# Reordering the head of a gated mixture-of-experts attention kernel: keys ahead of x, weight maxima in two rounds, weight halves at other places

## What is computed

```python
# xattn(batch=ctx, latent=layernorm(x))
weights = softmax((latent @ Wq.T) @ (batch @ Wk.T).T / sqrt(128))
x = x + tanh(g_xattn[0]) * weights @ (batch @ Wv.T)
# ffn(layernorm(x)), tokens n = 64*128, 4 blocks of sequences behave alike
logits = normalise(h) @ normalise(sim_matrix) - sigmoid(gates)
w = softmax(where(mask > 0, relu(logits), -inf))        # over the 16 experts
q = sum_e w[:, e] * (h @ q_proj[e])                     # k and v likewise
o = softmax(q @ k.T / sqrt(128)) @ v                    # within a sequence
x = x + tanh(g_ffn[0]) * sum_e (w[:, e] * o) @ o_proj[e]
```

## Time and profile before

| | |
|---|---|
| median of 3 runs | 885.28 us (885.21 to 885.91) |
| time of the profiled execution | 885.93 us |
| its span, first to last instruction | 884.1 us |
| TensorE products | 828.6 us busy, 94% of the span |
| VectorE | 613.5 us, 69% |
| GpSimd | 552.1 us, 62% |
| ScalarE | 519.3 us, 59% |
| mean granted TensorE clock | 0.992 |

### The profile page before, as it was taken

The page is one execution under the profiler, slowest core; times in us unless marked ns, Lnnn a source line. Parts: engine busy times, 40 slices in busy tenths (PEclk is TensorE's granted clock), DMA queues, the critical chain, the costliest instruction groups (busy, mean ns, idle before and its releaser), DMA issues.

```text
span 884.1 us, 16223 instructions
## 1 busy us (share of the span) xinstructions
PE 828.6 (94%) x4344; PEld 458.8 (52%) x4344; DVE 613.5 (69%) x1575; ACT 519.3 (59%) x1148; POOL 552.1 (62%) x588
## 2 busy tenths in 40 slices
PE   4579999999999999999999999999999999999976
PEld 3445555555555555555555555555555555545432
DVE  3777567777685867768676786867677676766545
ACT  3555657565665756566575656656575565656353
POOL 2264567575675757567575756657575765857464
PEclk9999999999999999999999999999999999999988
DMA  8753554453645555364654536464463636466342
GB/s 224 188 191 107 188 196 156 165 183 127 225 128 198 191 174 176 115 217 144 198 176 175 198 104 221 133 203 166 175 202 121 228 103 216 151 205 214 97 154 72
DMA packets 58531, 150.49 MB, mean 170 GB/s; under 512 B 5568, under 2 KB 22144, under 8 KB 58496
## 3 DMA queue, kind: packets, MB, share of 16 engines
q1 hardware_dynamic: 57776, 150.00, 50.3%
q10 hardware_dynamic: 720, 0.08, 0.1%
HBM read 145.34 MB, written 4.72 MB: 170 GB/s over the span
## 4 chain that ended last, share of the span: by engine, by line
PE 33%; issue 29%; POOL 28%; DVE 5%; ACT 3%; POOLq 1%; DMA 1%; ACTq 0%; DVEq 0%
POOL stage L457 13%; POOL zq L452 9%; PE acc_q L890 7%; PE acc_k L890 7%; PE acc_v L890 7%; PE acc_o L906 6%; POOL rstd L437 2%; POOL norm L446 1%; POOL rstd L425 1%; DVE zo_full L753 1%; DVE zq_full L743 1%; PE oT_p L982 1%; PE m L928 1%; PE m L1029 1%; DMA sim_sb<-in_L_ffn_sim_matrix_dram 1%
## 5 line engine op out<-in xcount | busy, mean ns | idle before, releaser
L452 POOL TENSOR_TENSOR zq<-zq_full,zq 128x512 f16<-128x512 f32 x192 | 224.8, 1172 | 218.6 <-ACT zq L505 218.6
L505 ACT ACTIVATE zq<-zq_full 128x512 f16<-128x512 f32 x256 | 161.0, 629 | 201.0 <-DVE zq_full L743 195.6
L457 POOL TENSOR_TENSOR stage<-zo_full,stage 128x512 f16<-128x512 f32 x208 | 240.7, 1160 | 58.2 <-ACT stage L513 58.2
L906 PE MATMUL acc_o<-stage,w_hi 128*128 128x512 f16 x512 | 195.8, 388 | 7.7 <-POOL stage L457 4.2
L743 DVE TENSOR_TENSOR zq_full<-wq_bc,x2T_p 128x512 f32<-128x512 f32 x256 | 173.2, 678 | 34.5 <-ACT x2T_p L606 29.8
L890 PE MATMUL acc_q<-zq,w_hi 128*128 128x512 f16 x512 | 194.5, 380 | 0.0
L890 PE MATMUL acc_k<-zq,w_hi 128*128 128x512 f16 x512 | 194.5, 380 | 0.0
L890 PE MATMUL acc_v<-zq,w_hi 128*128 128x512 f16 x512 | 194.3, 380 | 0.0
L753 DVE TENSOR_TENSOR zo_full<-stage,oT_p 128x512 f32<-128x512 f32 x256 | 172.5, 679 | 7.0 <-PE oT_p L982 6.4
L513 ACT ACTIVATE stage<-zo_full 128x512 f16<-128x512 f32 x256 | 160.0, 628 | 25.1 <-DVE zo_full L753 25.1
L906 PE MATMUL acc_o<-stage,w_lo 128*128 128x512 f16 x256 | 99.1, 387 | 0.0
(11 more groups left out here) (141 smaller groups left out, 1057.4 us busy)
## 6 DMA issues: line engine op xcount, KB each, us to landing
wq_bc<-w_rows SPq DMA_DIRECT2D x128, 512.0 KB, 4.8
stage<-w_rows SPq DMA_DIRECT2D x128, 512.0 KB, 3.7
out_dram<-x_all SPq DMA_DIRECT2D x16, 256.0 KB, 4.3
ctx_g<-in_ctx_dram SPq DMA_DIRECT2D x16, 154.0 KB
x_all<-in_x_dram SPq DMA_DIRECT2D x2, 256.0 KB, 6.8
x_all<-in_x_dram SPq DMA_DIRECT2D x1, 512.0 KB, 9.2
w_rows<-wT SPq DMA_DIRECT2D x16, 32.0 KB, 3.2
wq_sb<-in_L_xattn_Wq_dram SPq DMA_DIRECT2D x1, 64.0 KB, 5.6
```

Source lines behind the costliest of these rows:

```text
L452: nc.gpsimd.tensor_tensor(zq[:, 1, e % Z_SLOTS, :], zq_full[:, e % F_SLOTS, :], zq[:, 0, e % Z_SLOTS, :], ALU.subtract).then_inc(zq_lo_poo ...
L457: nc.gpsimd.tensor_tensor(zo[:, 1, e % Z_SLOTS, :], zo_full[:, e % F_SLOTS, :], zo[:, 0, e % Z_SLOTS, :], ALU.subtract).then_inc(zo_lo_poo ...
L505: nc.scalar.activation(zq[:, 0, e % Z_SLOTS, :], zq_full[:, e % F_SLOTS, :], ACT.Copy).then_inc(zq_hi_done, 1)
L906: last = nc.tensor.matmul(acc[O][:], w[:, O, e, :], zo[:, half, e % Z_SLOTS, :], start=(e == 0 and n == 0), stop=(e == E - 1 and n == 2))
```

## The change

On the loads: the second group's x is loaded behind `k_proj`. In pass -2, ScalarE copies the keys ahead of normalising x (step 7) and copies the transposed x at step 8, TensorE transposes x at step 8, and the small setup of both stands behind that. VectorE reduces q's weights ahead of its setup and k's behind it, ahead of the scores' maxima; its setup of the similarity matrix (`setup_sims`) moves to step 9; the second group's first statistics move to the end of the pass. `share_weight_max` and the chain of VectorE behind it get a turn: turn 0 for q, k and v at the end of pass -2, turn 1 for o in pass 0, with o's reduction at step 1, TensorE's part behind the experts of step 4, and VectorE's (`setup_out`) at the end of step 5. `HIGH_AT` and `LOW_AT` have other places. The diff, cut (not shown: new semaphores, a memset of `wmax`, VectorE's norm operations that move unchanged into `setup_sims`, the bodies of both `setup` that move unchanged):

```diff
-        HIGH_AT = [(-1, 2), (-1, 4), (-1, 8), (0, 1)]
-        LOW_AT = [(-1, 7), (-1, 9), (-1, 10), (0, 3)]
+        HIGH_AT = [(-2, 15), (-2, 15), (-1, 2), (0, 7)]
+        LOW_AT = [(-2, 15), (-1, 0), (-1, 6), (0, 9)]
...
                 sp.dma_start(stage[:, m], w.rearrange("e c h -> c e h")).then_inc(proj_in[m], 16)
-                if m == 0:
+                if m == K:
                     load_x(1)
...
GpSimd:
-                    if s == 11 and has(g1 + 1):
+                    if s == 1 and isinstance(i, int) and i == -1:
+                        first_rstd(g1)
+                    if s == 11 and has(g1 + 1) and not (isinstance(i, int) and i == -2):
                         first_rstd(g1 + 1)
...
ScalarE:
+            def setup():
+                act.wait_ge(small_in, 16 * 5)
+                nc.scalar.activation(sig[:], gates_b[:], ACT.Sigmoid)
+                nc.scalar.activation(tanh_x[:], gx[:], ACT.Tanh)
+                nc.scalar.activation(tanh_f[:], gf[:], ACT.Tanh).then_inc(tanh_done, 1)
+                act.wait_ge(tanh_done, 1)
+                act.wait_ge(prep_pe, 2)
+                nc.scalar.activation(wvT[:], acc[K][:, 0:P], ACT.Copy, scale=tanh_x[:]).then_inc(wvT_done, 1)
+                nc.scalar.activation(exp_0[:], tanh_f[:], ACT.Exp)
...
             def weight_high(m):
-                act.wait_ge(prep_dve, 5)
+                if m == O:
+                    act.wait_ge(out_prep, 1)
+                else:
+                    act.wait_ge(prep_dve, 5)
...
-                    if s == 3 and has(g1):
+                    if s == (7 if first else 3) and has(g1):
+                        if first:
+                            keys(g1)
...
-                    if s == 5 and has(g1):
+                    if s == (8 if first else 5) and has(g1):
                         wait(act, xnT_ps, g1 + 1)
                         wait(act, xscore_ps, g1)
                         nc.scalar.activation(xnT[:], m0[:], ACT.Copy).then_inc(xnT_sb, 1)
+                        if first:
+                            setup()
...
VectorE:
+            def share_max(turn, of):
+                step, n = prep_chain, 5 * turn
+                dve.wait_ge(wmax_ps, 2 * turn + 1)
+                nc.vector.tensor_reduce(wmax_t[:], acc[O][0:4, 0:P], AX_X, ALU.max).then_inc(step, 1)
+                dve.wait_ge(step, n + 1)
+                nc.vector.tensor_scalar(wmax_d[:], ident[0:4, 0:4], wmax_t[:], None, ALU.mult).then_inc(step, 1)
+                dve.wait_ge(wmax_ps, 2 * turn + 2)
+                nc.vector.tensor_scalar(wmax_all[:, of], acc[O][:, P:P + 4][:, of], 2.0 ** -60, 2.0 ** 60, ALU.max,
+                                        ALU.min).then_inc(step, 1)
...
             def setup_weights():
+                share_max(0, slice(Q, O))
+                nc.vector.tensor_scalar(w_up[:, Q:O], w_up[:, Q:O], W_UP, None, ALU.mult).then_inc(prep_dve, 1)
...
+            def setup_out():
+                share_max(1, slice(O, O + 1))
...
                 if first:
                     first_stats(0)
+                    dve.wait_ge(consts, 1)
+                    weight_max(Q)
                     setup()
-                    weight_max(Q)
+                    weight_max(K)
...
                     if s == 9 and first:
-                        weight_max(K)
-                    if s == 10 and has(g1 + 1):
+                        setup_sims()
+                    if s == 10 and has(g1 + 1) and not first:
                         first_stats(g1 + 1)
...
-                    if s == 11 and first:
+                    if s == 10 and first:
                         weight_max(V)
...
                     if s == 15 and first:
+                        setup_weights()
+                        first_stats(g1 + 1)
+                    if s == 1 and isinstance(i, int) and i == 0:
                         weight_max(O)
-                        setup_weights()
+                    if s == 5 and isinstance(i, int) and i == 0:
+                        setup_out()
...
TensorE:
-            def share_weight_max():
-                pe.wait_ge(wmax_done, 4)
...
+            def share_weight_max(turn):
+                pe.wait_ge(wmax_done, 3 + turn)
+                pe.wait_ge(prep_chain, 5 * turn)
+                nc.tensor.transpose(acc[O][0:4, 0:P], wmax[:], ident[:]).then_inc(wmax_ps, 1)
+                pe.wait_ge(prep_chain, 5 * turn + 2)
+                nc.tensor.matmul(acc[O][:, P:P + 4], ones[0:4, :], wmax_d[:],
+                                 start=True, stop=True).then_inc(wmax_ps, 1)
...
-                if isinstance(i, int) and i == -1:
-                    share_weight_max()
...
                         experts(i, s)
+                        if isinstance(i, int) and i == 0 and s == 4:
+                            share_weight_max(1)
...
-                    if s == 5 and has(g1):
+                    if s == (8 if first else 5) and has(g1):
                         wait(pe, xn_done, g1 + 1)
...
                         last.then_inc(xnT_ps, 1)
+                        if first:
+                            setup()
...
                         last.then_inc(att_ps, 1)
+                        if first:
+                            share_weight_max(0)
```

More of the change, by code:

```diff
@@ L514, in zo_high, with keys @@
                                      ACT.Copy).then_inc(zo_hi_done, 1)
+            def keys(g):
+                wait(act, kxT_ps, g + 1)
+                wait(act, xscore_ps, g)
+                nc.scalar.activation(kxT[:], m1[:, 0:G * S], ACT.Copy, scale=RSQRT_C).then_inc(kxT_sb, 1)
             def body(i):
                 g1, g2, gc, gd = i + 2, i + 1, i - 1, i - 2
+                first = isinstance(i, int) and i == -2
                 for s in range(E):
@@ L577, in body @@
                         nc.scalar.activation(ctxT[:], m1[:, 0:G * S], ACT.Copy).then_inc(ctxT_sb, 1)
[L578 to L581, removed]
+                    if s == 7 and has(g1) and not first:
+                        keys(g1)
                     if s == 8 and has(g2):
@@ L610, in body @@
                         nc.scalar.activation(pxT[:], m1[0:S, :], ACT.Copy).then_inc(pxT_sb, 1)
-                    if isinstance(i, int) and (i, s) in HIGH_AT:
-                        weight_high(HIGH_AT.index((i, s)))
+                    for m, at in enumerate(HIGH_AT):
+                        if isinstance(i, int) and (i, s) == at:
+                            weight_high(m)
             passes(act, body)
@@ new lines, in setup_sims @@
+            def setup_sims():
+                dve.wait_ge(nrm_root, 1)
+                nc.vector.tensor_scalar(sim_nrm[:], sim_nrm[:], 1e-12, None, ALU.max).then_inc(nrm_step, 1)
+                dve.wait_ge(nrm_step, 1)
+                nc.vector.reciprocal(sim_nrm[:], sim_nrm[:]).then_inc(nrm_step, 1)
+                dve.wait_ge(nrm_step, 2)
+                nc.vector.tensor_tensor(sn[:], sim_sb[:], sim_nrm[:], ALU.mult).then_inc(prep_dve, 1)
+            def share_max(turn, of):
[7 more added lines that the diff above has]
+                                        ALU.min).then_inc(step, 1)
+                dve.wait_ge(step, n + 3)
+                nc.vector.tensor_scalar(w_pow[:, of].bitcast(U32), wmax_all[:, of].bitcast(U32), 0x7F800000, None,
+                                        ALU.bitwise_and).then_inc(step, 1)
+                dve.wait_ge(step, n + 4)
+                nc.vector.reciprocal(w_up[:, of], w_pow[:, of]).then_inc(step, 1)
+                dve.wait_ge(step, n + 5)
@@ L855, in body @@
                             zo_low(g, e)
-                    if isinstance(i, int) and (i, s) in LOW_AT:
-                        weight_low(LOW_AT.index((i, s)))
+                    for m, at in enumerate(LOW_AT):
+                        if isinstance(i, int) and (i, s) == at:
+                            weight_low(m)
             passes(dve, body, x_in)
@@ L865, in _, with setup @@
             pe.wait_ge(consts, 1)
[L866 to L877 removed]
+            def setup():
+                pe.wait_ge(small_in, 16 * 5)
+                nc.tensor.transpose(acc[K][:, 0:P], wv_sb[:], ident[:]).then_inc(prep_pe, 1)
+                pe.wait_ge(prep_dve, 1)
+                nc.tensor.matmul(acc[V][:, 0:E], ones[:], sim_sq[:], start=True, stop=True).then_inc(prep_pe, 1)
+            def share_weight_max(turn):
[5 more added lines that the diff above has]
+                                 start=True, stop=True).then_inc(wmax_ps, 1)
             def experts(i, s):
```

53 lines of the change are left out of this document (11 added, 42 removed).

## The result

| | before | after |
|---|---|---|
| median of the runs | 885.45 us (4 runs, 885.21 to 885.91) | 893.75 us (4 runs, 892.99 to 894.53) |
| ratio, 95% interval | | 1.0091 (1.0077 to 1.0105) |
| profiled execution: time, span | 885.93, 884.1 us | 892.99, 891.2 us |

Slower by 8.3 us, or 0.9%; the prediction said 893.7. The profiled execution of after is the shortest of its four: its span is 7.1 us longer than that of before.

The account below looks back on a forecast made before the run. TensorE was taken to bound the kernel, so delays in the head or first QKV pass reach the end whole. Terms 0.9 - 0.4 + 6.5 - 0.5 + 1.9 = 8.4 us gave 893.7 us, range 889.5 to 897.2.

Parts of the forecast that it names:

- first expert's product later: Head: the reordered head shifts the first expert's product, now at 54.01 us, by +0.9, bounds +0.3 to +2.0.
- from there to the end of expert 4: First pass: o's w_hi no longer holds up x2T, so TensorE's 0.36 us idle ahead of the logits goes: -0.4.
- the wait: Behind expert 4: TensorE waits for wmax_d, queued behind group 1's gate chain on VectorE: +6.5 us, low bound 5.1.
- clock behind it: After TensorE's idle wait, a stretch of products runs at 1.2 GHz: +1.9 us, bounds 0 and 3.8.
- context copy done in time: After the wait: ScalarE has copies done that TensorE waited for at 74.40: -0.5 us.
- The balance of 3.2 lost and 2.3 given back: Head: w_rows written 3.2 us later, 2.3 of cover by VectorE's work given back, leaving +0.9.
- The trip of w_rows: Head: gate weights through memory take 1.9 + 4.0 us from write to landing, ending near 51.2.
- ScalarE's setup: Head: setup behind the key copy, with two table loads of 1.28 us, takes 3.5 us, 16.1 to 19.6.
- rival 3: Head: ScalarE's setup takes longer than its rows; with 2.6 us more the time is 896.3 us; chance 0.04.
- rival 2: First pass: the stall is there but the clock behind it stays up: 891.8 us; chance 0.10.
- rival 4: Behind expert 4: VectorE's two operations finish before TensorE arrives, so no wait: 885.8 us, no change; chance 0.04.
- rival 5: Later passes take the delay back, some 13 returning 11 us in all: 882.6 us, faster; chance 0.04.

Follow-up runs that it names:

- experiment 1: After, with the second maxima round's product moved from behind expert 4 to behind expert 7, VectorE's rest to step 8, o's halves two steps later: 886.2 us, 1.0006 to before.
- experiment 2: After, with VectorE's whole part of the second maxima round moved to step 4, ahead of gate_logits: 887.43 us, ratio 1.0017.
- Experiment 3: After, with 22 unread products of 512 columns on TensorE between the second round's transpose and product: 891.09 us, ratio 1.0062.
- experiment 4: Before, with only o's maximum moved to a second round in pass 0 and o's halves at (0, 7) and (0, 9): 892.93 us, ratio 1.0082.
- Experiment 6: The kernel of experiment 5 with the second group's statistics back at their old step: 884.99 us, ratio 0.9989.
- Experiment 7: The kernel of experiment 1 with the halves of q, k and v back at their old places: 885.37 us, ratio 0.9993.
- experiment 5: After, with one round of maxima including o and all halves at their old places, keeping the new head order and loads: 886.57 us, ratio 1.0003.
- experiment 8: The kernel of experiment 1 with the halves of q, k and v spread into the gaps of the gate chain: 883.89 us, ratio 0.9977.
- experiment 10: Before, with 11 unread fill products on TensorE ahead of the attention product at the end of the head: 884.72 us, ratio 0.9989.
- experiment 9 filled: Experiment 8 with three maxima rounds, halves moved and second context loaded earlier (882.31 us), plus 8 fill products ahead of the attention product: 883.26 us, 0.9971.
- experiment 8 filled: The kernel of experiment 8 with 8 unread fill products on TensorE ahead of the attention product: 884.53 us, ratio 0.9985.

## Why the prediction was right

The time was right, 893.7 against 893.75, and so was the mechanism. Term by term the trace is smaller than the sum, though: 6.5 us at the marker instead of 8.4. That the medians agree to the tenth is luck, as the list below shows.

| term | predicted | trace |
|---|---|---|
| first expert's product later | +0.9 | +0.20 (54.01 to 54.21) |
| from there to the end of expert 4 | -0.4 | -0.1 (67.22 to 67.29 in all) |
| the wait | +6.5 | +5.74 (67.29 to 73.03) |
| clock behind it | +1.9 | +1.5 (7 products, 0.21 each) |
| context copy done in time | -0.5 | -0.7 (no idle time at 81.01; from expert 5 to there 7.98, of which 1.5 is the clock, against 7.18 before) |
| sum | +8.4 | +6.6; marker +6.51 |

- **The head.** The balance of 3.2 lost and 2.3 given back held in kind: the idle time of VectorE ahead of the first scaled input is there, 2.32 us. The sizes were off because the early head was 0.6 us quicker (statistics done at 27.20, not 27.8) and the chain of the maxima took 1.96 instead of 2.2: normalising started at 32.90 rather than 34.0. The trip of w_rows, put at 1.9 + 4.0, took 6.3. My bounds missed both: the statistics came 0.8 earlier than before, where I had allowed 0.5, and the first product 0.20 later, where I had put at least 0.3. Experiments 1 to 3 have the same head, and their first product stands at 53.44, 53.50 and 54.09, so in four traces this term is -0.6 to +0.2.
- **ScalarE's setup** ended at 19.32, put at 19.6: two loads of 1.28 us, the next function 0.02 and 0.01 behind each, in the fence of the head above. The drain that the Trainium skill adds for a load ("ScalarE: Activation LUTs", "What ACT_TABLE_LOAD costs") doesn't show here either, and with it rival 3 falls.
- **Inside the pass.** Between the first expert and expert 4's end two things nearly cancel. Three more products at the start than before ran at 1.2 GHz (11, not 8), 0.6 us, which the prediction had not thought of. Against them TensorE's idle times ahead of the transposes of x and of the logits went: 0.35 us, which ended at 62.16 in the trace of before, and 0.36. The prediction had counted only the second. Together they give 0.20 + 0.63 - 0.35 - 0.36 = 0.12, where 0.07 was measured.
- **The wait** was the term that decides. Its place, its releaser (wmax_d) and its cause (the gate chain ahead in VectorE's queue) are as put. I had read the chain's length off group 1's chain before, 5.4 us; here it was 4.6 (67.33 to 71.9), since one operation was drawn out (`fb`, 0.94, while GpSimd worked from 69.76 to 70.91) and not two. The stall of 5.74 lies between my bounds, 5.1 and 6.5 (the terms of the lower one add to 5.0). Experiments 1, 2 and 4 show the term: without it 7.5 us come back, and alone it costs 7.2.
- **The clock** fell as put, 1.5 instead of 1.9. I had counted nine slow products in the first stretch of before, where eight are, since two of the ten in its window belong to the attention product. Experiment 3 shows 1.75 at the marker, 0.12 of it from an earlier head, and rival 2 falls.
- **Rivals 4 and 5.** TensorE did stop. Later passes returned nothing (6.51 at the first marker, 6.52 at the last).
- **What the markers leave.** They give 6.5, the spans 7.1, the medians 8.3. The profiled execution of after was the shortest of four that lie 1.5 us apart, and the profiled one of before the longest, by 0.5 over its median. So the medians add 1.2 to the spans' 7.1, and nothing in the prediction stands for that: its span, 892.5, is 1.3 too long. The number of slow products at the start differs too, 5 to 12 among the traces, at 0.21 us each. What else makes the spread of the executions was not measured.

Whether the change loses anything apart from the wait is not shown: the medians say 0.5 to 1.1 us, the markers a gain of 0.7 to 0.8, and experiment 1's interval includes 1. Experiment 6 shows a gain of the keys-first order of about 1 us. Experiment 7 points to the halves ahead of the gate as what takes it back, by a difference whose intervals overlap. The late statistics of the second group cost experiment 5 its gain, but not after: there GpSimd has `shift` ready at 36.92, and `xn` begins at 38.13, straight behind v's high half on ScalarE.

## What to carry to other kernels

A wait for two short operations lasts until everything that stands ahead of them in their engine's queue is done: before a cross-engine step is put into a stream that bounds the kernel, find when the other engine begins it, not how long it takes, and put some work of the waiting engine between the two (three experts took 7.5 us back here). A piece that is moved must be followed through every queue behind it: in experiment 5 the second group's statistics, put behind a reduction of 2.25 us on VectorE, held up ScalarE by way of GpSimd and took back all that the new order had won. Work that nobody waits for goes into the gaps of the critical chain, not ahead of it: the same halves, moved from ahead of the gate's normalising into the gaps behind it, were worth 2.3 us (experiments 1 and 8); moved behind it without regard to the gaps, they were worth 0.8 in the medians, with overlapping intervals (experiment 7).

## What the runs showed of the hardware

- A stretch at the lower clock costs its lost time only where TensorE has no later wait to absorb it: in experiment 10 eight expert products were 1.7 us quicker, and the next wait grew by 1.86, from 0.35 to 2.21. The attention product, on whose result that wait hangs, was 0.92 quicker, and the marker came 0.94 earlier.
- The length of the idle time did not by itself decide the clock behind it. Behind 8 fill products and 2.28 us of idle time it was at 0.50 (from 52.4 to 57.0, experiment 9 filled), behind 8 and 2.88 us it was up (attention product 1.16 us, expert products 0.22 apart, experiment 8 filled), and behind 22 and 0.22 us it stayed at 1.00. The 8 products took 2.41 us in the first of these and 1.89 in the second. What made the difference is open.
- The time from the write of the 32 KB of gate weights to the issue of the first load behind it was 1.9 to 2.4 us in the kernels without fill at the end of the head and 3.3 to 3.5 in the three with it (41.92 to 45.37, 40.81 to 44.27, 41.09 to 44.35). Nothing that I changed in these kernels touches those transfers, and the fill products start only behind that issue (46.71, 45.31, 45.89). It was seen only, and its cause is open, and so is why experiment 8's filled version gained 0.4 at the marker and nothing in its runs, which lie between 882.83 and 886.0.
